# Opening of a token, attention and FFN layer: the first two pairs of sequences in another order, and two vector operations in another form

## The chip, the cores and the metric

One Trainium2 chip, one of its cores. The metric is the device time of one execution in microseconds. The kernel before took 981.53 us as the median of three runs (979.28 to 981.59).

## What is computed

Two layers over 32 sequences of 192 tokens (64 image patches and 128 words), 256 channels, all in float32. The change lies in layer 0 only:

```python
h = concat([patches(x) @ tokW + tokb, table[x_txt]], axis=1)
a = layernorm(h)
q, k, v = a @ wq.T, a @ wk.T, a @ wv.T
h = h + softmax(causal(q @ k.T / 16)) @ v
a = layernorm(h)
h = h + ternary_linear(gelu(ternary_linear(a, w_up)), w_down)
# ternary_linear: x / (rms(x) + eps) times sign(w) * (|w| > 0.5 * mean|w|)
```

Layer 1 (a recurrent mixer and a mixture of experts) follows in the stages B and C of the program and is left alone.

## The kernel before

Stage A (`part_a`) computes layer 0. It takes the sequences two at a time: 16 pairs, numbered 0 to 15 here, each as three tiles of 128 tokens (both sequences' image tokens in one tile, then the words of each). A float32 product is made of products of a high part, rounded to the short format of TensorE, and a low part, the rest: hi times hi, hi times lo, lo times hi (`three`, `product`). So most results leave the accumulator (PSUM) twice: ScalarE (ACT) writes the high part (`hi`), VectorE (DVE) subtracts it for the low part (`lo`). For the patches VectorE makes the high part (`patch_hi`), GpSimd (POOL) the low part (`patch_lo`); for the GELU outputs GpSimd makes the low part (`gelu_lo`, L334).

The steps of a pair are named by kind. In time they come as: `tok` (patch product), `emb` (add the bias, statistics), `root1` (powers on GpSimd), `apply1` (writes x_normed), `xT` (six transposes, "turn"), `x_split`, `t` (times the merged query-key matrix), `t_split`, `score`, `max`, `exp`, `pT`, `v`, `v_split`, `pv`, `h1` (residual and second statistics), `root2`, `scale2` (writes x_normed of the second norm), `x2T`, `x2_split`, `up.0` to `up.7` with `gelu.0` to `gelu.7` and `add.0` to `add.7` (sums of squares), `down.0` to `down.2`, `ss`, `rscale`, `h2`.

One list `order`, written by hand, sets the order on all engines: `run` goes through it once for every step g from -4 to 15, and `offset` says for each kind how many pairs ahead of g it works (tok 2, v and pv 1, up and down 0). Each engine executes its own pieces in that order and waits on semaphores, and never skips a waiting instruction. The steps from -4 to 1 and from 12 to 15 are written out; a loop makes the ones between. The attention of pair 0 falls in step -2, pair 0's probabilities and pair 1's scores in step -1, the FFN of pair 0 in step 0.

The steps before 0 also prepare weights. On VectorE `abs_sum` sums a weight matrix's magnitudes, TensorE adds them over the partitions (`[128 x 1]` product), and `ternary` writes half the mean (`half_alpha`) and then each half of the ternary matrix, in two instructions each (L478, L481), with `gelu_sq` as a scratch tile. `raw_Wl` and `raw_Wv` are the tiles in which the up and down weights lie here. TensorE executes extra transposes of the identity, called fills (L716, table `fill`), ahead of some steps of the opening. ACT_TABLE_LOAD is ScalarE's change between the tables of exp and GELU.

In `patch_load` SyncE (SP) loads the next pair's patches once both halves of the last ones are split. The first down product of pair 0 waits for the whole of the down weights:

```python
if c == 0 and isinstance(n, int) and n == 0:
    pe.wait_ge(s["w_sum"], 4)
```

and pair 1's patches are split on VectorE behind pair 0's statistics and ahead of its `apply1`:

```python
last.then_inc(s["ln_aggr"], 1)
if isinstance(n, int) and n == 0:
    patch_hi(1)
```

## Time and profile before

| | us |
|---|---|
| median of three runs | 981.53 |
| lowest and highest run | 979.28, 981.59 |
| the profiled execution: its own time | 979.7 |
| its span | 977.8 |
| TensorE (PE) busy in the span | 934.9 |
| VectorE (DVE) busy | 791.8 |
| ScalarE (ACT) busy | 594.2 |
| GpSimd (POOL) busy | 545.2 |

The profile covers one execution. A timeline row gives the start and the duration in us, the engine and the line, the tiles written and read, how many equal neighbours it merges (x3), and in brackets how long the engine had stood idle before it and what ended that. Engines followed by q are their queues. Products of TensorE overlap, so that 12 of them can start in 1.5 us though each lasts 0.3.

### The profile page before, as it was taken

The page shows a single profiled execution, that of the slowest core. Times are in us where ns is not written, and L with a number is a line of the kernel's source. Part 1 is how long each engine was busy: PE and PEld are TensorE (multiplying, and loading weights), DVE is VectorE, ACT ScalarE, POOL GpSimd, SP SyncE. Part 2 cuts the span into 40 slices and gives each one's busy share as a digit, 9 for nine tenths or more (in the row PEclk, how much of TensorE's full clock was granted, in tenths as well). Part 3 has the DMA queues.
Part 4 walks back from the last instruction along what each step waited for, and adds up shares of the span by engine and source line. Part 5 has one row for each costly group of instructions (what it writes and reads, how often), then busy time and mean ns, then how long its engine had stood idle before and what let it go on. Part 6 is the DMA issues. An engine that isn't in the chain of part 4 may idle for free. (4 is left out here: it accounts for less than half of the span.)

```text
span 977.8 us, 19833 instructions
## 1 busy us (share of the span) xinstructions
PE 934.9 (96%) x6016; PEld 837.6 (86%) x6016; DVE 791.8 (81%) x2376; ACT 594.2 (61%) x1183; POOL 545.2 (56%) x675
## 2 busy tenths in 40 slices
PE   6889999999999999988899999999999999998998
PEld 6789999999999999875678888888888888877887
DVE  4878877777778777774589999999999989995787
ACT  1366666666666666664666767667767766752442
POOL 4256666666666666444445545455455456552673
PEclk9999999999999999999999999999999999999999
DMA  6001111111111113003799899999999999992310
GB/s 226 17 28 44 45 44 44 43 43 43 43 43 43 43 57 128 17 17 113 94 146 153 151 155 158 153 151 152 167 153 173 180 166 154 153 140 52 121 65 22
DMA packets 63014, 96.35 MB, mean 99 GB/s; under 512 B 12366, under 2 KB 32982, under 8 KB 62294
## 3 DMA queue, kind: packets, MB, share of 16 engines
q1 hardware_dynamic: 61390, 91.19, 50.1%
q0 software_dynamic: 1536, 4.20, 1.5%
q8 instruction: 37, 0.61, 0.3%
q14 instruction: 43, 0.35, 0.2%
q10 hardware_dynamic: 8, 0.00, 0.0%
HBM read 31.91 MB, written 13.11 MB: 46 GB/s over the span
## 5 line engine op out<-in xcount | busy, mean ns | idle before, releaser
L334 POOL TENSOR_TENSOR gelu_lo<-gelu_out,gelu_hi 128x384 fp32r<-128x384 f32 x124 | 146.0, 1205 | 29.2 <-DVE gelu_hi L549 28.7
L1050 POOL TENSOR_TENSOR B_y<-B_scan_in,B_states 128x512 f32<-128x512 f32 x48 | 61.8, 1288 | 84.8 <-ACT B_states L1139 84.8
L752 PE MATMUL psAB<-ternary_down,gelu_hi 128*128 128x256 f32 x384 | 96.9, 291 | 5.3 <-POOL gelu_lo L334 4.5
L688 PE MATMUL psAB<-x2T_hi,ternary_up 128*128 128x384 f32 x256 | 92.7, 362 | 0.8 <-DVE residual L678 0.6
L752 PE MATMUL psAB<-ternary_down,gelu_lo 128*128 128x256 f32 x384 | 93.4, 282 | 0.0
L688 PE MATMUL psAB<-x2T_lo,ternary_up 128*128 128x384 f32 x256 | 86.1, 336 | 0.0
L1317 PE MATMUL psAB<-Win_hi,B_x_hi 128*128 128x512 f32 x192 | 83.5, 435 | 0.0
L752 PEld LDWEIGHTS psAB<-ternary_down,gelu_hi 128*128 128x128 f32 x384 | 72.2, 188 | 9.7 <-POOL gelu_lo L334 8.0
L1062 POOL TENSOR_TENSOR B_decayed_u<-B_scan_in 128x512 f32<-128x512 f32 x48 | 62.1, 1293 | 29.5 <-DMA B_scan_in<-B_stage 28.2
L1235 DVE SCALAR_TENSOR_TENSOR psAB<-B_decayed_u,psAB 128x128 f32<-128x128 f32 x192 | 67.8, 353 | 12.1 <-PE psAB L1329 11.2
L1329 PEld LDWEIGHTS psAB<-B_partial_dots,B_minus_same_batch 128*128 128x128 f32 x384 | 65.3, 191 | 14.3 <-DVE B_partial_dots L1219 4.1
L1317 PE MATMUL psAB<-Win_hi,B_x_lo 128*128 128x512 f32 x192 | 75.5, 393 | 0.0
L1317 PE MATMUL psAB<-Win_lo,B_x_hi 128*128 128x512 f32 x192 | 75.3, 392 | 0.0
L752 PEld LDWEIGHTS psAB<-ternary_down,gelu_lo 128*128 128x128 f32 x384 | 72.5, 189 | 0.0
L1056 POOL TENSOR_TENSOR B_v_scale<-B_half_vv,half_powers 128x1 f32<-128x1 f32 x48 | 26.3, 549 | 78.8 <-ACT B_v_squared L1160 78.8
L403 ACT ACTIVATE gelu_out<-psAB 128x384 f32<-128x384 f32 x128 | 62.7, 490 | 10.2 <-PE psAB L688 9.9
L1219 DVE CUSTOM_DVE_ANT_0 B_products<-B_scan_in,psAB 128x128 f32<-128x128 f32 x192 | 55.2, 287 | 13.4 <-DVE psAB L1235 8.0
L1224 DVE TENSOR_TENSOR psAB<-psAB,B_scan_in 128x128 f32<-128x128 f32 x192 | 57.5, 299 | 6.5
L568 DVE TENSOR_TENSOR gelu_sq_sum<-gelu_sq_sum,gelu_sq 128x384 f32<-128x384 f32 x105 | 61.2, 582 | 1.7
L1329 PE MATMUL psAB<-B_partial_dots,B_minus_same_batch 128*128 128x1 f32 x384 | 54.8, 212 | 3.9 <-DVE B_partial_dots L1219 3.6
L1342 PE MATMUL psAB<-Wout_hi,B_y_hi 128*128 128x256 f32 x192 | 55.6, 290 | 2.7 <-DVE B_y_lo L1279 1.5
L390 ACT ACTIVATE gelu_sq<-gelu_out 128x384 f32<-128x384 f32 x112 | 57.3, 528 | 0.0
(274 smaller groups left out, 3318.2 us busy)
## 6 DMA issues: line engine op xcount, KB each, us to landing
B_scan_in<-B_stage SPq DMA_DIRECT2D x192, 256.0 KB, 6.9
patches<-in_patches SPq DMA_DIRECT2D x16, 384.0 KB, 3.1
B_residual<-layer_out SPq DMA_DIRECT2D x48, 128.0 KB, 4.1
out_dram<-B_residual SPq DMA_DIRECT2D x48, 128.0 KB, 3.7
layer_out<-residual SPq DMA_DIRECT2D x32, 128.0 KB, 1.8
raw_Win<-in_experts SPq DMA_DIRECT2D x3, 768.0 KB, 4.2
raw_Wl<-in_experts SPq DMA_DIRECT2D x3, 768.0 KB, 4.2
layer_out<-residual SPq DMA_DIRECT2D x32, 64.0 KB, 2.0
```

The lines of the kernel that those rows point to most:

```text
L334: nc.gpsimd.tensor_tensor(act_l[:, k, :], act[:, k % DEEP, :], act_h[:, k, :].bitcast(F32), ALU.subtract).then_inc(s["ffn_lo"], 1)
L390: nc.scalar.activation(out, act[:, k % DEEP, :], ACT.Square).then_inc(s["sq_done"], 1)
L403: nc.scalar.activation(act[:, k % DEEP, :], ps[:, 6 + k % 2, 0:GT], ACT.Gelu).then_inc(s["gelu_done"], 1)
L568: nc.vector.tensor_tensor(sqsum[:], sqsum[:], sq[:, k % DEEP, :], ALU.add).then_inc(s["sqsum_done"], 1)
L688: last = nc.tensor.matmul(out, a, b, start=(n == 0), stop=(n == len(terms) - 1))
L752: last = nc.tensor.matmul(ps[:, 6 + k // 2, (k % 2) * D:(k % 2 + 1) * D], x[:, c, k * P:(k + 1) * P], dn_w[:, c, :], start=(c == 0 and x i ...
L1050: nc.gpsimd.tensor_tensor(y[:, j % 2], ring[:, j % R_RING, :, GATE, :], hs[:, j % 2], ALU.mult).then_inc(s["y"], 1)
L1062: nc.gpsimd.tensor_tensor(lu[:, j % 2], ring[:, j % R_RING, :, LAM, :], ring[:, j % R_RING, :, U, :], ALU.mult).then_inc(s["lu"], 1)
L1224: nc.vector.tensor_tensor(state(j, k), state(j, k), ring[:, j % R_RING, k, DRIVE, :], ALU.subtract).then_inc(s["scan"], 1)
L1235: nc.vector.scalar_tensor_tensor(out=state(i, k), in0=lu[:, i % 2, k, :], scalar=dot[:, t % 2:t % 2 + 1], in1=state(i, k), op0=ALU.mult, o ...
L1317: last = nc.tensor.matmul(out, a, b, start=(not biased and ks[0] == 0 and n == 0), stop=(ks[-1] == DC - 1 and n == len(terms) - 1), skip_g ...
L1329: nc.tensor.matmul(dot[:, t % 2:t % 2 + 1], minus[:], part[:, t % 2:t % 2 + 1], start=True, stop=True).then_inc(s["dot"], 1)
```

## The change

- `order_of` gives steps -2, -1 and 0 lists of their own. A third number moves a piece to a later pair. v and v_split of pair 0 now come in step -2 ahead of its scores, those of pair 1 in step -1 ahead of pair 1's scores, and are gone from step 0. The second half of ternary_up and the split of pair 2's patches come later in step -1 than before. x_split of pairs 1 and 2 gets a wait for the scores.
- The sum of the down weights and ternary_down (`abs_down`, `tern_down`) move from step -1 to step 0; the scratch tile of `ternary` is now the weight stage.
- `tok` of pair 0 goes by kind: six hi times hi, six with the patches' low part, six with the weights' low part, each with its own waits. Pair 1's goes to bank 6 and no longer waits for max.
- `emb` of pair 0 takes the statistics of the words ahead of the patches' product.
- The warm-up of the GELU table for pair 0 becomes one of exp.
- x_normed of both norms, in all pairs, and the low parts of the weights (`chunk_lo`) become scalar_tensor_tensor, with the per-token factor as a broadcast second input.
- Other numbers of fills: 46 at the start, then 6, 14, 8, 10, 12 and 6.

```diff
         offset = {...
-                  "abs_down": 1, "tern_down": 1,
+                  "abs_down": 0, "tern_down": 0,
...
+        order_of = {
+            -2: [... """ids_load.0.0 tok.0.0 merge.0.0 patch_load.0.0
...
+            -1: [... """ids_load.0.0 exp.0.0 gelu_table.0.0 pT.0.0
...
+            0: [(w, k, 0) for w, k in order if w not in ("v", "v_split")]}
...
-                for kind, k in order:
-                    off = offset.get(kind, 1)
+                for kind, k, forward in order_of.get(g, ()) if isinstance(g, int) and g in order_of else [
+                        (kind, k, 0) for kind, k in order]:
+                    off = offset.get(kind, 1) + forward
...
-                    nc.scalar.activation(warm_gelu[:], ones[:, 0:1], ACT.Gelu).then_inc(s["gelu_warmed"], 1)
+                    nc.scalar.activation(warm_gelu[:], ones[:, 0:1], ACT.Exp if isinstance(n, int) and n == 0 else ACT.Gelu
+                                         ).then_inc(s["gelu_warmed"], 1)
...
+                    if isinstance(n, int) and n in (1, 2):
+                        sc.wait_ge(s["score_done"], n)
...
+                        v.wait_ge(text_in[sl], 32 * (half + 1))
+                        for i in (1, 2):
+                            nc.vector.bn_stats(stats[:, i, :], emb[:, sl, i, :])
...
-                        last = nc.vector.tensor_scalar(xn[:, i, :], emb[:, sl, i, :], moments[:, i, 0:1],
-                                                       rstd[:, i:i + 1], ALU.subtract, ALU.mult)
+                        last = nc.vector.scalar_tensor_tensor(out=xn[:, i, :], in0=emb[:, sl, i, :],
+                                                              scalar=moments[:, i, 0:1],
+                                                              in1=rstd[:, i:i + 1].to_broadcast([P, D]),
+                                                              op0=ALU.subtract, op1=ALU.mult)
...
-            fill = {("tok", 0): 40, ("xT", 0): 16, ("t", 0): 10, ("score", 0): 10, ("pv", 0): 10, ("xT", 1): 4,
-                    ("t", 1): 10, ("score", 1): 10}
+            fill = {("tok", 0): (46, 6), ("xT", 0): (6, 6), ("t", 0): (14, 6), ("pT", 0): (8, 7), ("pv", 0): (10, 7),
+                    ("t", 1): (12, 7), ("x2T", 0): (6, 7)}
...
+                        pe.wait_ge(s["patch_hi"], 1)
+                        for a, b, ready, parts in ((pat_h, tok_h, s["w_hi"], 2), (pat_l, tok_h, s["patch_lo"], 1),
+                                                   (pat_h, tok_l, s["w_lo"], 2)):
+                            for c in range(KPC):
+                                if c == 0 or (c == 4 and parts == 2):
+                                    pe.wait_ge(ready, 1 + c // 4)
```

VectorE at the end of step -1, before the change: behind the low part of t of pair 1 (ternary_down, then scale2 of pair 0; `ln_roots` are the powers from GpSimd).

```order
L472 TENSOR_SCALAR half_alpha<-psAB 128x1 [waits A_w_alpha_ps]
L478 TENSOR_SCALAR gelu_sq<-raw_Wv,half_alpha 128x1024 [waits A_w_sum,A_w_alpha]
L481 SCALAR_TENSOR_TENSOR ternary_down<-raw_Wv,half_alpha,gelu_sq 128x1024 [waits A_w_sign]
L478 TENSOR_SCALAR gelu_sq<-raw_Wv,half_alpha 128x1024 [waits A_w_sum]
L481 SCALAR_TENSOR_TENSOR ternary_down<-raw_Wv,half_alpha,gelu_sq 128x1024 [waits A_w_sign]
L664 SCALAR_TENSOR_TENSOR ln_den<-ln_roots 128x3 [waits A_ln2_roots]
L667 RECIPROCAL ln_scale<-ln_den 128x3 [waits A_ln2_den]
L671 TENSOR_SCALAR x_normed<-residual,ln_moments,ln_scale 128x256 [waits A_ln2_scale]
```

The same engine in step 0 after the change, from GELU output 0 to the low part of t of pair 2 and on.

```order
L568 CAST gelu_hi<-gelu_out 128x384 [waits A_gelu_done] x2
L655 SCALAR_TENSOR_TENSOR x_normed<-embedded,ln_moments,ln_rstd 128x256 [waits A_xT_done,A_ln_aggr,A_ln_rstd]
...
L484 TENSOR_REDUCE abs_sum_parts<-raw_Wv 128x32 [waits A_tern_in1]
L487 TENSOR_REDUCE abs_sum<-abs_sum_parts 128x1 [waits A_w_abs_parts]
L568 CAST gelu_hi<-gelu_out 128x384 [waits A_gelu_done]
...
L560 TENSOR_TENSOR tT_lo<-psAB,tT_hi 128x768 [waits A_t_hi]
L493 TENSOR_SCALAR half_alpha<-psAB 128x1 [waits A_w_alpha_ps]
L499 TENSOR_SCALAR weight_stage<-raw_Wv,half_alpha 128x1024 [waits A_w_sum,A_w_alpha]
L502 SCALAR_TENSOR_TENSOR ternary_down<-raw_Wv,half_alpha,weight_stage 128x1024 [waits A_w_sign]
L499 TENSOR_SCALAR weight_stage<-raw_Wv,half_alpha 128x1024 [waits A_w_sum]
L502 SCALAR_TENSOR_TENSOR ternary_down<-raw_Wv,half_alpha,weight_stage 128x1024 [waits A_w_sign]
```

The sum of the down weights and ternary_down now stand among the splits of pair 0's GELU outputs and pair 2's attention.

TensorE in step 0 after the change, the waiting products between t of pair 2 and the first down products of pair 0 (psAB is the accumulator).

```order
L719 MATMUL psAB<-xT_hi,qk_hi 128x384 [waits A_emb_img,A_x_lo]
...
L763 MATMUL psAB<-abs_sum,ones 128x1 [waits A_h1_done,A_w_abs]
L789 MATMUL psAB<-ternary_down,gelu_hi 128x256 [waits A_ffn_lo,A_w_sum,A_gelu_done]
L789 MATMUL psAB<-ternary_down,gelu_lo 128x256
L789 MATMUL psAB<-ternary_down,gelu_hi 128x256 [waits A_ffn_lo]
```

The product with abs_sum stood in step -1 before, ahead of pair 1's scores; now it stands directly ahead of the down products.

VectorE in step -2 after the change, from pair 0's patch product to x_normed.

```order
L636 TENSOR_TENSOR embedded<-psAB,patch_bias 128x256 [waits A_tok_done,A_mask_ready,A_const_in]
L641 BN_STATS ln_stats<-embedded 128x6 [waits A_emb_img,A_text_in0]
L646 BN_AGGR ln_moments<-ln_stats 128x2 [waits A_ln_stats]
...
L556 CAST patches_hi<-patches 128x768 [waits A_tok_done,A_patch_in]
L655 SCALAR_TENSOR_TENSOR x_normed<-embedded,ln_moments,ln_rstd 128x256 [waits A_ln_aggr,A_ln_rstd]
```

The cast of pair 1's patches stands where it stood, ahead of x_normed.

## Rows read from the trace of the kernel before

**Rows 1.** A stretch: PE, PEld, DVE, ACT, POOL busy us; granted clock, DMA share, GB/s.
```profile
124.00:408.00 284.00, 280.59 (x2084) 271.79 (x2082) 223.23 (x634) 181.99 (x383) 190.74 (x188) 1.00 0.16 49
```
**Rows 2.** Waits of PE from 80 to 400 us: in total, times, longest.
```profile
PE psAB L752 <- POOL gelu_lo L334: 2.6, 12, 0.3
```
**Rows 3.** Timeline of DVE, around pair 0's first x_normed.
```profile
17.66 0.56 DVE L537 CAST patches_hi<-patches 128x768 fp32r<-128x768 f32 x1 [1.49 <-DMA patches<-in_patches]
18.14 2.56 DVE L628 TENSOR_SCALAR x_normed<-embedded,ln_moments,ln_rstd 128x256 f32<-128x256 f32 x3
```
**Rows 4.** Line L271, the loads of patches, first 60 us.
```profile
DMA to landing us min/median/max: 3.0/3.2/8.5
```
**Rows 5.** Timeline of PE: turns, t, score, down and the turn of pair 1.
```profile
20.75 0.87 PE L699 MATMUL psAB<-ident,x_normed 128*128 128x128 f32 x6 [2.39 <-DVE x_normed L628]
23.52 0.44 PE L688 MATMUL psAB<-xT_hi,qk_hi 128*128 128x384 f32 x1 [0.80 <-DVE xT_lo L541]
27.77 0.39 PE L688 MATMUL psAB<-xT_hi,tT_hi 128*128 128x256 f32 x1 [0.30 <-DVE tT_lo L541]
43.65 0.45 PE L688 MATMUL psAB<-xT_hi,qk_hi 128*128 128x384 f32 x1 [0.80 <-DVE xT_lo L541]
53.57 1.54 PE L699 MATMUL psAB<-ident,x_normed 128*128 128x128 f32 x6 [3.25 <-DVE x_normed L671]
72.75 0.39 PE L752 MATMUL psAB<-ternary_down,gelu_hi 128*128 128x256 f32 x1
77.37 0.87 PE L699 MATMUL psAB<-ident,x_normed 128*128 128x128 f32 x6
```
**Rows 6.** Busy us by engine in one stretch, granted clock behind them.
```profile
53.70:56.50 2.80, 2.80 (x14) 2.80 (x15) 1.52 (x8) 1.35 (x4) 0.00 (x0) 0.50 0.00 0
```
**Rows 7.** The same for the fills (L716) alone: PE, PEld, clock.
```profile
2.00:5.00 3.00, 3.00 (x14) 3.00 (x15) 1.00 0.53 145
6.00:8.00 2.00, 2.00 (x21) 1.98 (x19) 1.00 1.00 313
```
**Rows 8.** Timeline of POOL: patches_lo, the powers of scale2, the first gelu_lo.
```profile
18.30 1.90 POOL L318 TENSOR_TENSOR patches_lo<-patches,patches_hi 128x768 fp32r<-128x768 f32 x1 [0.71 <-DVE patches_hi L537]
46.97 1.78 POOL L359 TENSOR_TENSOR ln_roots<-ln_pair,half_powers 128x6 f32<-128x6 f32 x1
61.95 1.98 POOL L334 TENSOR_TENSOR gelu_lo<-gelu_out,gelu_hi 128x384 fp32r<-128x384 f32 x2
```
**Rows 9.** Line L628, x_normed: duration of one, ns.
```profile
L628 DVE TENSOR_SCALAR x_normed<-embedded,ln_moments,ln_rstd x48: 399/406/1891, 18.1 to 390.7; 128x256 f32<-128x256 f32 x48
```
**Rows 10.** Line L562, scalar_tensor_tensor of the last pair, two inputs in on-chip memory.
```profile
L562 DVE SCALAR_TENSOR_TENSOR gelu_sq_sum<-gelu_sq_sum,gelu_sq x7: 550/558/1371, 437.1 to 445.4; 128x384 f32<-128x384 f32 x7
```
**Rows 11.** Timeline of DVE from 31 to 73 us.
```profile
31.50 0.17 DVE L605 TENSOR_SCALAR neg_max<-row_max 128x3 f32<-128x3 f32 x1
38.41 1.05 DVE L628 TENSOR_SCALAR x_normed<-embedded,ln_moments,ln_rstd 128x256 f32<-128x256 f32 x3
39.38 2.29 DVE L463 TENSOR_REDUCE abs_sum_parts<-raw_Wv 128x32 f32<-128x2048 f32 x1
47.76 0.15 DVE L472 TENSOR_SCALAR half_alpha<-psAB 128x1 f32<-128x1 f32 x1
52.05 0.16 DVE L664 SCALAR_TENSOR_TENSOR ln_den<-ln_roots 128x3 f32<-128x3 f32 x1
58.56 0.42 DVE L610 TENSOR_TENSOR embedded<-psAB,patch_bias 128x256 f32<-128x256 f32 x1
64.76 0.35 DVE L549 CAST gelu_hi<-gelu_out 128x384 fp32r<-128x384 f32 x1
67.60 0.96 DVE L541 TENSOR_TENSOR xT_lo<-psAB,xT_hi 128x768 fp32r<-128x768 f32 x1 [1.01 <-ACT xT_hi L379]
69.77 1.25 DVE L641 SCALAR_TENSOR_TENSOR residual<-psAB,row_inv,embedded 128x256 f32<-128x256 f32 x3
72.24 0.31 DVE L652 BATCH_NORM_AGGREGATE ln_moments<-ln_stats 128x2 f32<-128x6 f32 x3
```

More of the change, by code:

```diff
@@ L145, in flat, with tok_bank @@
             return t[:].rearrange("p a b -> p (a b)")
+        def tok_bank(n):
+            return 6 if isinstance(n, int) and n == 1 else 2
         chunks = []
@@ L606, in piece @@
                 if kind == "emb":
+                    first = isinstance(n, int) and n == 0
+                    if first:
+                        v.wait_ge(text_in[sl], 32 * (half + 1))
+                        for i in (1, 2):
+                            nc.vector.bn_stats(stats[:, i, :], emb[:, sl, i, :])
+                        v.wait_ge(s["const_in"], 16)
+                        v.wait_ge(s["mask_ready"], 1)
                     v.wait_ge(s["tok_done"], n + 1)
                     wait(v, s["h1_done"], n - 1)
-                    nc.vector.tensor_tensor(emb[:, sl, 0, :], ps[:, 2, 0:D], bias_tok[:], ALU.add).then_inc(s["emb_img"], 1)
+                    nc.vector.tensor_tensor(emb[:, sl, 0, :], ps[:, tok_bank(n), 0:D], bias_tok[:],
+                                            ALU.add).then_inc(s["emb_img"], 1)
                     v.wait_ge(text_in[sl], 32 * (half + 1))
                     v.wait_ge(s["emb_img"], n + 1)
-                    for i in range(TILES):
+                    for i in (0,) if first else range(TILES):
                         last = nc.vector.bn_stats(stats[:, i, :], emb[:, sl, i, :])
@@ L670, in piece @@
                     for i in range(TILES):
-                        last = nc.vector.tensor_scalar(xn2[:, i, :], h[:, sl, i, :], moments2[:, i, 0:1],
-                                                       scale2[:, i:i + 1], ALU.subtract, ALU.mult)
+                        last = nc.vector.scalar_tensor_tensor(out=xn2[:, i, :], in0=h[:, sl, i, :],
+                                                              scalar=moments2[:, i, 0:1],
+                                                              in1=scale2[:, i:i + 1].to_broadcast([P, D]),
+                                                              op0=ALU.subtract, op1=ALU.mult)
                     last.then_inc(s["ln2_out"], 1)
@@ L706, in keys @@
                 return x[:, k, :].rearrange("p (t c) -> p t c", t=TILES)[:, 0:3:2, :]
-            fill = {("tok", 0): 40, ("xT", 0): 16, ("t", 0): 10, ("score", 0): 10, ("pv", 0): 10, ("xT", 1): 4,
-                    ("t", 1): 10, ("score", 1): 10}
+            fill = {("tok", 0): (46, 6), ("xT", 0): (6, 6), ("t", 0): (14, 6), ("pT", 0): (8, 7), ("pv", 0): (10, 7),
+                    ("t", 1): (12, 7), ("x2T", 0): (6, 7)}
             def piece(kind, k, n, sl, half):
-                if isinstance(n, int):
-                    for _ in range(fill.get((kind, n), 0)):
-                        nc.tensor.transpose(ps[:, 6, 0:P], ident[:], ident[:])
+                if isinstance(n, int) and (kind, n) in fill:
+                    turns, into = fill[kind, n]
+                    if into == 7:
+                        pe.wait_ge(s["w_alpha"], 1)
+                    for _ in range(turns):
+                        nc.tensor.transpose(ps[:, into, 0:P], ident[:], ident[:])
                 if kind == "merge" and isinstance(n, int) and n == 0:
@@ L734, in piece @@
                             pe.wait_ge(s["w_sum"], 2)
+                            pe.wait_ge(s["emb_img"], 2)
                     else:
```

43 lines of the change are left out of this document (28 added, 15 removed).

## The prediction

> **What bounds the kernel now.** First the busy time by stretches. Between 124 and 408 us TensorE is busy 280.6 of 284 us at the full clock [rows 1], and its only wait there, 2.6 us in 12 pieces, is for the last `gelu_lo` that GpSimd subtracts [rows 2]. So the 14 later pairs stand near TensorE's bound, with 0.2 us a pair set by GpSimd and VectorE. What is left to win lies before 80 us, where a chain runs from engine to engine, so I read the timelines of that stretch next: what each instruction waits for last, and where VectorE stands idle. I number pairs from 0; x_normed(0) is pair 0's. At the end I count along VectorE's queue, since the change fills it.
>
> **Part 1, patch products by kind, bank 6 for pair 1.** The product of pair 0 can begin when its high parts are there and end some 2.5 us earlier. But the next step is not free to follow: VectorE splits pair 1's patches ahead of x_normed(0), and that cast ends an idle wait for a DMA, at 17.66 [rows 3]. The load takes 8.5 us to land, the longest of its four [rows 4], behind the ternary weights on the same engines, and the change moves none of it. So x_normed(0) starts at 18.14 as before: this part is worth 0 while that load holds. Its cost is the idle TensorE behind it. It now has nothing from about 13.6 (46 fills to 8.9, 18 products to 11.1, merge and 6 fills 2.5; an estimate) to 20.8, 7.2 us instead of 2.4 [rows 5]. After the idle 3.3 us ahead of the turn of pair 0's second norm the granted clock was 0.50, the 1.2 GHz level, to 56.6, 3.1 us, and six turns took 1.54 instead of 0.87 us [rows 5, 6]. A turn or fill then takes 0.2 us instead of 0.12. I take the same 3.1 us here: six turns to 22.05, 9.5 of the 14 fills slow, 4.5 fast, so t(0) at 24.5 against 23.52 [rows 5]: **+1.0**. Bounds: 0 if the clock holds, +1.8 if it stays low longer.
>
> Fills are transposes, and 21 ran in the 2 us from 6 us on, 14 in the 3 us from 2 us on, with nothing else on the engine [rows 7]: transposes alone brought the fast rate. The Trainium skill, "TensorE: Matmul & The Clock Gate", Part 4: PE-mode transpose, says that transposes do not count as busy for the clock. By it the low stretch would run on through all of t(0) and the sum would be about 2 us worse; the trace speaks against it, and I go by the row.
>
> **Part 2, tensor_scalar and tensor_tensor become scalar_tensor_tensor.** x_normed(0) takes 2.56 us for three since one sits 1.9 us behind GpSimd's patches_lo [rows 3, 8, 9]. A scalar_tensor_tensor with both inputs in on-chip memory is held in the same way: the seven of the last pair take 0.558 us and one of them 1.371, beside a `gelu_lo` [rows 10]. So I count no relief, and the length only: 0.558 less a third of 384 columns (0.13, from 0.4 for the 384 and 0.155 around them) is 0.425 against 0.406 of now [rows 9, 10], 0.02 each. Bounds: a gain of 1.5 us if GpSimd does not hold it; the same kind takes 1.25 us for three where it reads PSUM (the residual of [rows 11]), against 1.05 for pair 1's x_normed now [rows 11], 0.2 more a step of three. For tokW_lo the answer is the same, and its end is covered by 12 other products.
>
> **Part 3, v(0) ahead of score(0).** From t(0) to score(0) it is 4.25 us now [rows 5]. Then it is t (2.1), the alpha sum (0.3) and 18 value products at 0.12 (2.2), which outlast the split of t: 4.65, so score(0) at 29.15 against 27.77, **+1.4**. In return everything up to t(1) is shorter. neg_max is ready 3.9 us after the score starts (31.67 after 27.77 [rows 5, 11]), 33.05; then v_lo 0.95, and the embedding of pair 1 begins at 34.0; its powers are done 3.4 us on, 37.4 (58.56 to 61.95 [rows 8, 11]); x_normed(1) 1.2, half of ternary_up 2.05, xT_lo 1.0 and t(1) starts at 41.75 against 43.65 [rows 5]: **-1.9**. The two ACT_TABLE_LOADs fall away beside this chain, so they add nothing of their own.
>
> **Part 4, ternary_down and its sum leave the opening.** Now the powers of the second norm end at 48.75, and scale2 starts at 52.05, since 4.3 us of ternary_down stand before it [rows 8, 11]. Without them it starts at 46.9 and x2T(0) at 48.95 behind six fills, against 53.57 [rows 5]: **-4.6**. That is the change's profit, and it is partly kept from pair 2: patches_hi(2) moved behind scale2, so its patches_lo ends at 50.85, the load of the next patches goes out only then, lands 3.2 us later, as the middle ones do [rows 4], and its cast stands ahead of pair 2's embedding on VectorE: 54.6 against 58.56 [rows 11], **-4.0**.
>
> **Part 5, where that work went: VectorE in the first FFN step.** Down(0) on TensorE waits for the last ternary_down. Count VectorE from 54.6. Powers at 58.0. x_normed(2) then waits 1.0 us for the gelu_lo that starts with it (1.98 for two [rows 8]): 60.1. abs_sum of the down weights, 2.29 and 0.2 [rows 11]: 62.6 for gelu_hi 2, now at 64.76. From there to the residual h1(1) it is 5.0 us, 1.5 of them waits that fall away: 66.1 (69.77 now). Its statistics, 2.8 (69.77 to 72.55): 68.9. tT_lo, 0.95: 69.8. ternary_down, 4.3 (47.76 to 52.05): **74.1** [rows 11]. So the lead of 4.0 is spent, since 6.8 us of work joined an engine that is then full. TensorE is done with t(2) at about 67.6 and idle for 6.5 us. It starts down(0) at 74.2. Now it has 36 products left at 72.75 and reaches x2T(1) at 77.37 [rows 5], 0.122 us each with the full clock. Then it has 50: 6.1 us, and 1.25 more for 3.1 us at 0.50 (0.2 us each, 14 in 2.8 us [rows 6]). x2T(1) at 81.5 against 77.37: **+4.2**. Taking v(1) out of this step saves TensorE 2.2 us, all inside that idle time. Nothing later is idle enough to win it back: TensorE waits 0.2 us a pair.
>
> **Part 6, the 14 later pairs.** x_normed of either norm stands in the loop that sets the 0.2 us wait: gelu_hi 2 follows the first, the turn of the second follows the other. At 0.02 each and six a pair that is 0.12; a third of it I take as slack of the turn, so +0.08 a pair, **+1.1** in all. Bounds: -0.3 a pair (TensorE's whole idle share, 3.4 us in 284 [rows 1]) if the hold is gone, +0.38 if each step takes 1.25.
>
> **Sum.** +4.2 +1.1 = +5.3 on the profiled execution: span 977.8 to 983.1, time 979.7 to 985.0. That execution is 1.8 us under the median of the runs, 981.53, so I predict **986.8 us**.
>
> **Rivals.**
> A. *Not slower: the new x_normed runs beside GpSimd unhindered.* Place: the three overlaps (18.3, 58.0, and gelu_lo 1 of each pair). Price: -1.55 at 18.3, -1.0 at 58.0, and TensorE's idle share of 14 pairs, 0.3 each, -4.2, in place of +1.1. 4.2 - 2.55 - 4.2 = -2.55: 979.0. Slower turns into no change once 2.4 us are saved, which the first two places alone would do. For it: the residual of pair 1, of the new kind, took 1.25 us for three [rows 11] while GpSimd was subtracting, but it reads PSUM. Against: the row of 1.371 us. The Trainium skill, "SBUF — State Buffer", Who interferes with whom, says that a VectorE instruction with two SBUF inputs contends with a GpSimd instruction that reads SBUF; by that rule, which that row bears out, A does not come. Chance 0.20.
> B. *The patches of pair 1 land by 14 us.* Then part 1 does bring something: x_normed(0) ends at 16.9, still beside patches_lo(1), everything moves by -3.85, and VectorE's load in the FFN step leaves +0.3 + 1.1: 983.0. Against: issue and bytes are the same. Chance 0.13.
> C. *Each new x_normed is as long as the ones that read PSUM.* 14 x 0.38 = 5.3 instead of 1.1: 991.0. Chance 0.12.
> D. *Low clock through t(0)*, by the rule above: +2.1: 989. Chance 0.05.
> The forecast has 0.50.
>
> **How the numbers follow.** A measurement of this kernel can tell about 0.3%, 2.9 us, from no change: below 978.6 is faster, above 984.4 slower. Of the forecast's 0.50, 0.42 is slower; its 0.08 below the line is the case that the clock holds at 20.8 and 74 (-1.0, -1.25). A: 0.08 faster, 0.12 same. B: 0.03, 0.08, 0.02. C and D: slower. Together faster 0.11, same 0.28, slower 0.61. The range takes in A at its foot, 979.5, and C at its head, 991.5; the forecast alone would be 983.5 to 989.
>
> **What would show it.** patches_hi(1) still at 17.7 behind a DMA, x_normed(0) ending near 20.8; the clock at 0.50 from about 21 to 24; x2T(0) near 49; a VectorE without gaps from 55 to 74; TensorE idle for 6 us ahead of the first down product, with ternary_down as releaser, and the clock low after it; x2T(1) near 81.5; from there on pairs of the present length. I am wrong if down(0) starts before 71, which needs VectorE's embedding of pair 2 before 51.5, or if the later pairs change by more than 0.1 us each.

## The result, and the profile after

The changed kernel takes **992.37 us**, the median of 4 runs (991.01 to 993.97), beside 981.56 us (979.28 to 983.18) of the kernel before on the same chip. The ratio is 1.0108, with a 95% interval of 1.0083 to 1.0133: slower by 10.6 us, and slower than the range of the prediction reached. One run of e15 below, 1131 us long at a granted clock of 0.75, was in a slower state and is left out of all medians and ratios. The profiled execution took 991.01 us, its span is 988.9 against 977.8 us. The lines of the code have moved: x_normed of the first norm is L655, of the second L700, the split into low parts L560, the casts of the GELU L568, ternary L499 and L502, the turns L730, the products L719 and the down products L789.

The timeline of PE after: the turns of the first two pairs, the first product of t(1), of t(2) and of down(0). Columns: start us, duration us, engine, line, operation, tiles, shape, count, and in brackets the idle time before with what ended it.

```profile
21.14 1.54 PE L730 MATMUL psAB<-ident,x_normed 128*128 128x128 f32 x6 [7.13 <-DVE x_normed L655]
...
40.44 0.82 PE L730 MATMUL psAB<-ident,x_normed 128*128 128x128 f32 x6
...
43.21 0.44 PE L719 MATMUL psAB<-xT_hi,qk_hi 128*128 128x384 f32 x1 [0.64 <-DVE xT_lo L560]
...
50.36 0.82 PE L730 MATMUL psAB<-ident,x_normed 128*128 128x128 f32 x6
...
62.07 0.87 PE L730 MATMUL psAB<-ident,x_normed 128*128 128x128 f32 x6 [1.04 <-DVE x_normed L655]
68.70 0.69 PE L719 MATMUL psAB<-xT_hi,qk_hi 128*128 128x384 f32 x1 [3.46 <-DVE xT_lo L560]
78.57 0.55 PE L789 MATMUL psAB<-ternary_down,gelu_hi 128*128 128x256 f32 x1 [6.11 <-issue]
...
86.04 0.82 PE L730 MATMUL psAB<-ident,x_normed 128*128 128x128 f32 x6
```

Against [rows 5] it reads: xT(0) 0.4 us later, t(1) 0.4 us earlier, x2T(0) 3.2 us earlier, and x2T(1), the last row, 8.7 us later. All of that 8.7, and the 3.2 besides, goes between 50 and 86 us: 3.5 us of idle TensorE ahead of t(2), and 6.1 ahead of the first down product, which the profile puts down to no engine ("issue").

The timeline of DVE after tells what it was:

```profile
17.79 0.56 DVE L556 CAST patches_hi<-patches 128x768 fp32r<-128x768 f32 x1 [2.46 <-DMA patches<-in_patches]
18.27 2.82 DVE L655 SCALAR_TENSOR_TENSOR x_normed<-embedded,ln_moments,ln_rstd 128x256 f32<-128x256 f32 x3
...
48.31 1.27 DVE L700 SCALAR_TENSOR_TENSOR x_normed<-residual,ln_moments,ln_scale 128x256 f32<-128x256 f32 x3
...
55.63 0.42 DVE L636 TENSOR_TENSOR embedded<-psAB,patch_bias 128x256 f32<-128x256 f32 x1
...
59.23 2.79 DVE L655 SCALAR_TENSOR_TENSOR x_normed<-embedded,ln_moments,ln_rstd 128x256 f32<-128x256 f32 x3
61.94 2.27 DVE L484 TENSOR_REDUCE abs_sum_parts<-raw_Wv 128x32 f32<-128x2048 f32 x1
...
65.09 1.15 DVE L568 CAST gelu_hi<-gelu_out 128x384 fp32r<-128x384 f32 x1
...
66.63 1.15 DVE L568 CAST gelu_hi<-gelu_out 128x384 fp32r<-128x384 f32 x1
67.70 0.94 DVE L560 TENSOR_TENSOR xT_lo<-psAB,xT_hi 128x768 fp32r<-128x768 f32 x1
...
69.20 1.26 DVE L670 SCALAR_TENSOR_TENSOR residual<-psAB,row_inv,embedded 128x256 f32<-128x256 f32 x3
...
73.23 0.96 DVE L560 TENSOR_TENSOR tT_lo<-psAB,tT_hi 128x768 fp32r<-128x768 f32 x1 [1.24 <-ACT tT_hi L396]
...
77.19 1.29 DVE L502 SCALAR_TENSOR_TENSOR ternary_down<-raw_Wv,half_alpha,weight_stage 128x1024 fp32r<-128x1024 f32 x1
```

The last half of ternary_down ends at 78.48 and down(0) starts at 78.57. The busy time and the clock by stretches, TensorE alone (stretch, its length, busy us and instructions, granted clock, DMA share, GB/s):

```profile
14.00:17.00 3.00, 0.01 (x1) 0.98 0.85 339
17.00:21.00 4.00, 0.00 (x0) 0.50 0.01 2
21.00:24.00 3.00, 2.86 (x14) 0.50 0.66 194
24.00:27.00 3.00, 3.00 (x13) 0.50 0.09 30
27.00:28.00 1.00, 1.00 (x7) 0.93 0.00 0
...
68.00:71.00 3.00, 2.30 (x7) 0.52 0.01 3
71.00:74.00 3.00, 1.46 (x8) 0.91 0.01 3
74.00:78.00 4.00, 0.00 (x0) 0.62 0.13 36
78.00:81.00 3.00, 2.43 (x11) 0.50 0.13 40
```

The clock falls while TensorE is idle at 17 us, and TensorE then works at the 1.2 GHz level for 6 us from 21 on, and for some 3 us each behind the wait that begins at 65 us and the one that ends at 78.6.

The rest of the loss is in the later pairs. Of x_normed there, first after, then before: the groups of VectorE between 130 and 400 us (count, then busy us, mean ns, idle before).

```profile
L655 DVE SCALAR_TENSOR_TENSOR x_normed<-embedded,ln_moments,ln_rstd 128x256 f32<-128x256 f32 x30 | 16.5, 602 | 0.0
L700 DVE SCALAR_TENSOR_TENSOR x_normed<-residual,ln_moments,ln_scale 128x256 f32<-128x256 f32 x33 | 14.1, 481 | 0.4
```

```profile
L628 DVE TENSOR_SCALAR x_normed<-embedded,ln_moments,ln_rstd 128x256 f32<-128x256 f32 x33 | 14.8, 501 | 0.0
L671 DVE TENSOR_SCALAR x_normed<-residual,ln_moments,ln_scale 128x256 f32<-128x256 f32 x30 | 10.6, 410 | 0.4
```

And the waits of PE from 80 to 410 us, where [rows 2] has 2.6 us in 12:

```profile
PE psAB L789 <- POOL gelu_lo L351: 4.6, 10, 0.5
PE psAB L719 <- DVE xT_lo L560: 1.4, 2, 0.7
```

Measured from turn to turn of the second norm, pairs 1 to 14 (13 steps), a pair takes 25.36 us against 25.10. I use these two numbers for every run below: x2T(1), the start of the turn of pair 1's second norm, which takes in the whole opening, and the length of a later pair.

### The profile page after: what moved, and what is told of

It is laid out like the page before. It is cut to its first block and busy times, and to the rows that moved or that the text cites. A ratio compares the mean times of both kernels' runs of the same rounds, so it can differ in the third digit from the quotient of the medians.

```text
span 988.9 us, 19815 instructions
## 1 busy us (share of the span) xinstructions
PE 934.7 (95%) x6008; PEld 838.1 (85%) x6008; DVE 808.2 (82%) x2376; ACT 593.3 (60%) x1181; POOL 540.9 (55%) x675
## 5 line engine op out<-in xcount | busy, mean ns | idle before, releaser
L351 POOL TENSOR_TENSOR gelu_lo<-gelu_out,gelu_hi 128x384 fp32r<-128x384 f32 x124 | 144.0, 1187 | 36.6 <-DVE gelu_hi L568 36.1
L789 PE MATMUL psAB<-ternary_down,gelu_hi 128*128 128x256 f32 x384 | 98.2, 293 | 13.5 <-POOL gelu_lo L351 6.6
L789 PE MATMUL psAB<-ternary_down,gelu_lo 128*128 128x256 f32 x384 | 94.7, 284 | 0.0
L719 PE MATMUL psAB<-x2T_hi,ternary_up 128*128 128x384 f32 x256 | 92.8, 363 | 1.2 <-DVE residual L709 0.6
L789 PEld LDWEIGHTS psAB<-ternary_down,gelu_hi 128*128 128x128 f32 x384 | 73.3, 191 | 17.3 <-POOL gelu_lo L351 9.5
L719 PE MATMUL psAB<-x2T_lo,ternary_up 128*128 128x384 f32 x256 | 86.2, 337 | 0.0
L1366 PE MATMUL psAB<-Win_hi,B_x_lo 128*128 128x512 f32 x192 | 75.5, 393 | 0.0
L1111 POOL TENSOR_TENSOR B_decayed_u<-B_scan_in 128x512 f32<-128x512 f32 x48 | 62.2, 1295 | 22.3 <-DMA B_scan_in<-B_stage 12.4
L789 PEld LDWEIGHTS psAB<-ternary_down,gelu_lo 128*128 128x128 f32 x384 | 73.5, 191 | 0.0
L420 ACT ACTIVATE gelu_out<-psAB 128x384 f32<-128x384 f32 x128 | 62.6, 490 | 12.5 <-PE psAB L719 10.6
L475 ACT ACTIVATE x2T_hi<-psAB 128x768 fp32r<-128x768 f32 x16 | 13.0, 813 | 81.6 <-PE psAB L730 81.6
L1378 PE MATMUL psAB<-B_partial_dots,B_minus_same_batch 128*128 128x1 f32 x384 | 54.6, 211 | 3.8 <-DVE B_partial_dots L1268 3.5
```

Of the source, the lines that this page charges most:

```text
L351: nc.gpsimd.tensor_tensor(act_l[:, k, :], act[:, k % DEEP, :], act_h[:, k, :].bitcast(F32), ALU.subtract).then_inc(s["ffn_lo"], 1)
L420: nc.scalar.activation(act[:, k % DEEP, :], ps[:, 6 + k % 2, 0:GT], ACT.Gelu).then_inc(s["gelu_done"], 1)
L719: last = nc.tensor.matmul(out, a, b, start=(n == 0), stop=(n == len(terms) - 1))
L789: last = nc.tensor.matmul(ps[:, 6 + k // 2, (k % 2) * D:(k % 2 + 1) * D], x[:, c, k * P:(k + 1) * P], dn_w[:, c, :], start=(c == 0 and x i ...
L1111: nc.gpsimd.tensor_tensor(lu[:, j % 2], ring[:, j % R_RING, :, LAM, :], ring[:, j % R_RING, :, U, :], ALU.mult).then_inc(s["lu"], 1)
L1366: last = nc.tensor.matmul(out, a, b, start=(not biased and ks[0] == 0 and n == 0), stop=(ks[-1] == DC - 1 and n == len(terms) - 1), skip_g ...
```

## The experiments

I held three theories. **T1:** ternary_down and its sum in the first FFN step hold down(0) back. **T2:** the new form of x_normed costs the later pairs. **T3:** x_normed(0) behind the cast of patches(1) leaves TensorE idle, and the low clock after it makes t(0) late. Each ratio is against the kernel before, timed beside it; the median of before was 979.8 to 982.0 us in these groups of runs, so the ratios compare and the medians of different rows only roughly. x2T(1) and the pair are read from one execution each. The same kernel gave x2T(1) at 73.51 and 74.18 (e8, e15) and at 74.52 and 73.56 (e12, e16), so a difference of less than 1 us in that column says little.

| run | x2T(1), us | a later pair, us | median, us | ratio and interval |
|---|---|---|---|---|
| before | 77.37 | 25.10 | 981.6 | 1 |
| changed | 86.04 | 25.36 | 992.4 | 1.0108 (1.0083 to 1.0133) |
| e1, ternary_down back | 81.48 | 25.37 | 987.7 | 1.0075 (1.0049 to 1.0100) |
| e2, tensor_scalar back | 85.53 | 25.10 | 988.5 | 1.0077 (1.0052 to 1.0102) |
| e3, long fill | 86.77 | 25.38 | 991.4 | 1.0116 (1.0089 to 1.0143) |
| e4, cast behind | 83.99 | 25.38 | 989.4 | 1.0088 (1.0062 to 1.0113) |
| e5, before, new form | 78.98 | 25.33 | 986.0 | 1.0061 (1.0042 to 1.0081) |
| e6, e1 + e2 + e4 | 78.15 | 25.09 | 979.9 | 0.9994 (0.9977 to 1.0010) |
| e7, before, cast behind | 78.50 | 25.10 | 979.7 | 0.9992 (0.9975 to 1.0009) |
| e8, before, late half, fill | 73.51 | 25.10 | 976.8 | 0.9967 (0.9953 to 0.9982) |
| e9, e6 laid apart | 76.03 | 25.11 | 977.5 | 0.9956 (0.9938 to 0.9973) |
| e10, e9 with the short fill | 76.94 | 25.10 | 977.2 | 0.9959 (0.9941 to 0.9976) |
| e11, sum of down back | 86.16 | 25.33 | 992.3 | 1.0104 (1.0078 to 1.0131) |
| e12, e8 without the fill | 74.52 | 25.10 | 975.5 | 0.9931 (0.9904 to 0.9958) |
| e13, whole tile as input | 79.38 | 25.35 | 986.3 | one run |
| e14, one pointer scalar | 76.98 | 24.99 | 977.0 | one run |
| e15, e8 again | 74.18 | 25.10 | 976.0 | 0.9946 (0.9928 to 0.9964) |
| e16, e12 again | 73.56 | 25.11 | 976.3 | 0.9952 (0.9939 to 0.9966) |

### The three causes, one at a time (e1 to e4)

e1 puts ternary_down back into step -1, as before; its `[128 x 1]` product goes with it and no longer waits for the residual:

```diff
-    t_split.0.0 v.0.1 score.0.0 scale2.0.0      (step -1)
+    t_split.0.0 tern_down.0.1 tern_down.1.1 v.0.1 score.0.0 scale2.0.0
-    tern_up.1.-1 pv.0.0
+    tern_up.1.-1 abs_down.0.1 pv.0.0
```

> The changed kernel with ternary_down and its sum of magnitudes put back into step -1, everything else as changed. T1 (these five VectorE instructions in step 0 hold the first down product back): x2T(0) starts at about 57 us instead of 50.4, but down(0) no longer waits at 72 to 78.5, and x2T(1) comes at about 79 us instead of 86.0; the time falls by 6 to 8 us, to about 985. T2 (the new form of x_normed alone costs the time, 3.5 us over the steady pairs) and T3 (the long low clock behind x_normed(0)) leave x2T(1) at 85 us or later and the time within 1.5 us of 992.4.

x2T(1) came at 81.48: 4.6 of the 8.7 us, not 7, and the time fell by 0.33 points, 3.2 us. x2T(0) was at 55.61, 5.2 later than in the changed kernel, and down(0) at 75.5. T1 holds, for a little over half of the loss at x2T(1) and a third of the lost time; the 6 to 8 us that I expected were too much. e2 undoes the form in both norms (`tensor_scalar(xn, emb, moments, rstd, subtract, mult)` again):

> The changed kernel with tensor_scalar and its two pointer scalars back in both x_normed, everything else as changed. T2 (the form is slower by itself): the three instructions take 1.28 us again instead of 1.5 or more in the steady pairs, the pair from x2T to x2T goes from 25.36 to 25.10 us, and the time falls by 3.3 to 3.9 us, to about 988.8. Rival (the steady pair is longer for another reason, such as the phase in which the first pairs leave the queues): the pair stays at 25.3 or more and the time within 1 us of 992.4. What my prediction said of this, 0.08 us a pair, would give a fall of 1.1 us.

The pair is at 25.10 again, x2T(1) 0.5 us earlier, the time 0.31 points lower, 3 us. The first down product came 1.6 us earlier (77.00), but the granted clock behind it was at 0.50 until 82.6 us, 5.6 us on, where in the changed kernel it was so for 3.2 us (78.6 to 81.8), and TensorE took 8.5 us from there to x2T(1) instead of 7.5. T2 holds, and the length of the steady pair has no other cause. e4 moves one call:

```diff
                 last.then_inc(s["ln_aggr"], 1)
-                if n == 0: patch_hi(1)
...
             (apply1) last.then_inc(s["ln_out"], 1)
+                if n == 0: patch_hi(1)
```

> The changed kernel with the cast of patches(1) behind x_normed(0) on VectorE instead of ahead of it, everything else as changed. T3 (x_normed(0) waits behind a cast that waits for a transfer): x_normed(0) starts at about 15.3 us instead of 18.3 and takes 1.3 to 1.5 us instead of 2.8, as GpSimd is not yet on patches_lo(1); TensorE is idle for 2.5 us instead of 7, t(0) starts about 4 us earlier and the time falls by 3 to 4 us, to about 989. Rival (patches(1) is then what is late: its products end later and emb(1) takes the gain back): x_normed(1) at 38.7 us as now, and the time within 1 us of 992.4.

xT(0) came 3.1 us earlier, at 18.03, and x2T(1) 2.05 earlier; the time fell by 0.2 points, 2 us. Here too the first down product gained more, 3.0 us (75.52), but the clock was at 0.50 until 81.0 us and 8.5 us lay behind it instead of 7.5. In the timeline of DVE of e4 the wait for GpSimd has moved with the order, to wv_lo, 0.68 us long in the changed kernel:

```profile
16.70 1.28 DVE L653 SCALAR_TENSOR_TENSOR x_normed<-embedded,ln_moments,ln_rstd 128x256 f32<-128x256 f32 x3 [1.45 <-POOL ln_rstd L361]
17.89 0.55 DVE L556 CAST patches_hi<-patches 128x768 fp32r<-128x768 f32 x1
18.36 0.68 DVE L605 SCALAR_TENSOR_TENSOR qk_lo<-psAB,qk_hi 128x512 fp32r<-128x512 f32 x1
18.96 1.94 DVE L549 SCALAR_TENSOR_TENSOR wv_lo<-weight_stage,wv_hi 128x512 fp32r<-128x512 f32 x1
```

So the order takes x_normed off the load and off GpSimd, but VectorE has as much to do. e3 tests the other half of T3, `("xT", 0): (58, 6)` in place of `(6, 6)`:

> The changed kernel with 58 instead of 6 transposes of the fill ahead of xT(0), so that TensorE stays busy from 14.0 to about 21 us, while VectorE casts patches(1) and writes x_normed(0). T3 (the idle stretch brings the low clock, and transposes count as activity): the granted clock stays at the high level through t(0), t(0) starts 2 to 2.5 us earlier, and as the attention of step -2 is a chain, x2T(0) comes 1.5 to 2.5 us earlier; the time falls by 1 to 2.5 us. Rival (transposes don't hold the clock, as the Trainium skill says in "TensorE: Matmul & The Clock Gate", Part 4): the clock is at the low level from 17 to 27 us as now, and the time within 0.5 us of 992.4.

The stretches of PE of e3:

```profile
14.00:18.00 4.00, 4.00 (x39) 1.00 0.63 243
18.00:20.00 2.00, 2.00 (x20) 1.00 0.01 2
20.00:22.00 2.00, 0.09 (x1) 1.00 0.00 0
22.00:24.00 2.00, 1.83 (x17) 1.00 0.69 206
24.00:26.00 2.00, 1.64 (x12) 1.00 0.40 123
```

The clock stays at the full level over the whole of t(0), behind 58 transposes and nothing else from 13.6 to 20.1 us and 2.1 us of idle time. That is one execution, and no sure hold: in e9 below, 28 transposes to 16.1 us and 2.0 us of idle time ahead of xT(0) were followed by a stretch at 0.50, while the turns and the 14 fills behind them ran.

```profile
18.00:22.00 4.00, 3.81 (x20) 0.62 0.01 3
```

But there, as in e6 and e11, the clock came back to 1.00 (at 22.3, 21.8 and 25.2 us) before the first product of t(0) (22.97, 22.44, 25.74), when TensorE had executed only transposes since its wait. The hold in e3 and these returns go against the rule of the Trainium skill that I had weighed ("TensorE: Matmul & The Clock Gate", Part 4), though in the changed kernel the clock came back only 1.8 us into the products of t(0). And the time of e3 did not move. x2T(0) gained 0.9 us, and then the statistics of embedded(2) waited 2.0 us for the rows of its text (0.3 in the changed kernel), so that x2T(1) was at 86.77. The clock of the opening, which my Part 1 priced at 1 us, could be bought back and was worth nothing while that transfer and VectorE's queue stood behind it.

### The form alone, and all three together (e5, e6)

> The kernel before with nothing changed but the form: scalar_tensor_tensor with the broadcast input in both x_normed, in all 16 pairs. T2 (the form costs the steady pairs, and about the same in the opening): x2T(1) at 77.4 to 78.2 us, the pair at 25.36 instead of 25.10 us, and the time 3.3 to 4.5 us over that of before. Rival (the form costs only where the new order of the opening has put it beside GpSimd's work): under 1 us over that of before.

The kernel before with the new form alone is 0.61% slower, 6.0 us. In its profiled execution I find 1.6 by x2T(1), 13 x 0.23 = 3.0 in the steady pairs, and 1.5 in the last pair, of which more at the end. That is more than the 3 us that e2 gave back in the new opening, but the first is good to some 2 us and the second to 3.5, so the difference isn't shown.

> The changed kernel with three things put back or out of the way at once: both x_normed on tensor_scalar, the cast of patches(1) behind x_normed(0), ternary_down and its sum in step -1. If the causes are apart (T1, T2 and T3 hold side by side) their gains at x2T(1) add, 4.6 and 2.1 us and some 0.5 us of the form from 86.0 us, to 78.9 us, the pair is 25.10 us, and the time 10 to 11 us under that of the changed kernel, 0 to 1.5 us over that of before. Rival (they share one wait, so that the second removal finds little left): x2T(1) at 80.5 us or later, the time 3 us or more over that of before.

With all three in, the kernel is at the time of before (0.9994), x2T(1) 7.9 us earlier than in the changed kernel and 0.8 later than before. The single gains at x2T(1) were 4.6, 0.5 and 2.05, 7.1 us. Within the 1 us of that column they add, so they are three causes and not one wait seen three times. Two of them take a part of the change back. The third doesn't: the cast stands ahead of x_normed(0) in the kernel before as well, where moving it gains nothing (e7). The changed kernel with e1 and e2 alone wasn't run, so it isn't shown that those two parts of the change make up its whole loss. What is left of the change in e6 (products by kind, bank 6, values ahead of scores, no change of tables) brings no gain: xT(1) is at 37.09 instead of 40.94, and the waits of PE between 30 and 60 us say where that lead ends:

```profile
PE psAB L715 <- DVE xT_lo L560: 2.5, 1, 2.5
PE psAB L726 <- DVE x_normed L698: 2.3, 1, 2.3
PE psAB L715 <- POOL patches_lo L335: 1.5, 1, 1.5
```

### Where VectorE's work can stand (e7 to e12, e15, e16)

> The kernel before with the cast of patches(1) behind x_normed(0), nothing else. T3's wait is in this kernel too (the cast waits for its transfer at 17.66 us and stands ahead of x_normed(0)): x_normed(0) at about 17 us and 1.05 us long, its turns at about 18 instead of 20.75, and the time 2 to 3 us under that of before. Rival (the opening has other chains of the same length behind it, such as the raw weights' transfers and the products of pair 1, so that the attention of pair 0 gains nothing further on): x2T(1) within 0.7 us of 77.4 and the time within 1 us of before.

No gain. The profile is that of the slowest of its twelve runs (983.63 us). In it the products of pair 0 ended 0.75 us later than before, since the granted clock was at 0.50 from 11.6 us on (from 12.3 in before), and wv_lo took the hold as in e4. xT(0) was at 19.49; e12 and e16, with the same instructions up to there, had it at 18.03 and 18.07, without a low clock in those products. At x2T(0) 0.2 us were left, and the low clock there lasted to 59.3 us instead of 56.6. By the medians of 12 and 29 runs the cast alone is worth nothing here.

e8 adds two things: the second half of ternary_down behind the row maxima of pair 1, and 14 transposes ahead of x2T(0). The scratch tile of ternary moves to the weight stage with it. e12 is e8 without the transposes.

```diff
-    tern_up.0 tern_down.0 tern_down.1 add.4
+    tern_up.0 tern_down.0 add.4
-    x2T down.2 max tern_up.1
+    x2T down.2 max tern_down.1 tern_up.1
-    tern_tmp = sq[...]
+    tern_tmp = stage[:, 0:1024]
```

> The kernel before with the cast behind x_normed(0), the second half of ternary_down behind the row maxima of pair 1 instead of ahead of x_normed2(0) (its scratch in the weight stage), and 14 transposes ahead of x2T(0), so that TensorE doesn't stand idle there. If VectorE's chain to x_normed2(0) and the low clock behind its wait set the opening: x2T(0) 2 us earlier than in the run with the cast alone, no 0.50 clock at its turns (1.5 us in before), x2T(1) 2 to 3 us earlier, and the time 4 to 6 us under that of before. Rival (what comes behind, VectorE's queue of step -1 and 0, is as full as before, so the half is only moved): as the run with the cast alone, within 1 us.

> The kernel before with the cast behind x_normed(0) and the second half of ternary_down behind the row maxima of pair 1, but without the 14 transposes ahead of x2T(0). If the gain of the run with both is from the half (VectorE's order), x2T(1) is within 1 us of its 73.5 us and the time 2 to 3 us under that of before; if it is from the clock that the transposes hold, the clock is 0.50 for 3 us from about 50 us on, x2T(1) at 75 us or later and the time within 1.5 us of before.

Both are faster than before, 0.33% and 0.69%: 3.1 us where I had said 4 to 6 for e8, 6.1 where I had said 2 to 3 for e12. As e7 is no faster than before, the gain comes with the late half; the half without the cast wasn't run. The DVE timeline of e12 shows what it does: the second norm stands between the halves, and starts 2.8 us earlier than before. First e12, then the kernel before:

```profile
48.06 1.28 DVE L481 SCALAR_TENSOR_TENSOR ternary_down<-raw_Wv,half_alpha,weight_stage 128x1024 fp32r<-128x1024 f32 x1
...
49.67 1.06 DVE L671 TENSOR_SCALAR x_normed<-residual,ln_moments,ln_scale 128x256 f32<-128x256 f32 x3
...
52.65 1.28 DVE L481 SCALAR_TENSOR_TENSOR ternary_down<-raw_Wv,half_alpha,weight_stage 128x1024 fp32r<-128x1024 f32 x1
```

```profile
52.46 1.06 DVE L671 TENSOR_SCALAR x_normed<-residual,ln_moments,ln_scale 128x256 f32<-128x256 f32 x3
```

The turn at 50.78 has an idle time of 1.14 us before it instead of 3.25, and the clock there is at its full level without any transposes. To learn whether the transposes add something, both were timed again side by side:

> The kernel of e8 once more, beside that of e12: before, with the cast behind, the late half and 14 transposes ahead of x2T(0). If the clock at x2T(0) is worth what it showed in the profiles (x2T(1) 73.51 against 74.52 us): 1 us under e16. Otherwise within 0.5 us of e16.

> The kernel of e12 once more: before, with the cast behind and the late half, no transposes ahead of x2T(0). The time 3 to 6 us under that of before, as in e12 (6.1) and e8 (3.1 with the transposes).

976.0 and 976.3 us, 0.9946 and 0.9952: they add nothing that can be seen. This version, e16, beats both kernels: 5.6 us under before (0.48%, interval 0.34 to 0.61).

e9 lays the changed kernel's work out in the same way: e6, with the sum behind xT_lo(1), the first half behind the row maxima, the second behind v_lo(1), and longer fills, 28 ahead of xT(0) and 14 ahead of x2T(0). e10 has the six of the changed kernel ahead of xT(0) again, which its expectation calls none.

> The run with all three put back, with VectorE's work for ternary_down laid into its idle stretches instead of ahead of what TensorE waits for: the sum of magnitudes behind xT_lo(1), the first half behind the row maxima of pair 1, the second behind v_lo(1); besides 28 transposes (6 before) ahead of xT(0) and 14 (6) ahead of x2T(0). T1 in its strict form (what counts is not that VectorE does this work but which operand stands behind it): TensorE's 2.5 us ahead of t(1) and 2.3 us ahead of x2T(0) go, and with them the low clock at 42 to 46 us and 55 to 59 us; x2T(1) at 73 to 75 us instead of 78.15, the time 3 to 5 us under that of before. Rival (VectorE is full from 15 to 78 us, so what is moved is only paid elsewhere): x2T(1) at 77 us or later and the time within 1 us of before.

> The same kernel as e9 without any transposes ahead of xT(0). If transposes hold TensorE's clock over VectorE's wait (as the granted clock of 1.00 from 14 to 30 us in the run with 58 of them shows), the clock here is 0.50 for some 4 us from 17 us on, and x2T(1) and the time are 1 to 2 us later than in e9. Rival (VectorE's chain sets the start of t(0) and what follows at either clock): within 0.5 us of e9.

x2T(1) fell by 2.1 us against e6, to 76.03, and the time is 0.44% under before: the forecast of 3 to 5 us held, though x2T(1) is 1 us later than I said. TensorE's waits ahead of t(1) and x2T(0) went from 2.5 and 2.3 us to 0.6 and none. The time of e10 is the same within 0.3 us, so the rival holds for the fills once more. Its clock was not low from 17 us on as forecast, but from 23.4 to 26.8, under the products of t(0). The new order, at its best here, is no faster than the old order at its best (977.5 to 976.3): I find nothing that the change's reordering itself brings.

> The changed kernel with only the sum of magnitudes for ternary_down (2.46 us of VectorE) moved from step 0 to step -1, behind xT_lo(1); ternary_down itself stays in step 0. T1: VectorE has no idle time between x_normed(2) and h1(1) in step 0, so ternary_down ends about 2.4 us earlier than 78.5, less what x2T(0) is later; x2T(1) at 84 to 84.5 us instead of 86.0, the time 1.5 to 2 us under that of the changed kernel. Rival (down(0) waits for ternary_down's place behind tT_lo(1), whose chain through ScalarE sets it, not for VectorE's time): x2T(1) within 0.5 us of 86.0.

A miss. With only the 2.46 us of the sum taken out of step 0, x2T(1) was at 86.16 and the time as before that edit. xT(1) stood 0.3 us earlier than in the changed kernel, but x2T(0) 1.5 later, since the sum now stood ahead of the residual of pair 0. So ternary_down ended at 77.5, only 1 us earlier, and the low clock behind the wait for it, to 83.2 us, took that. Moving a part of the work ahead of the chain pays in one step what it saves in the other. T1 in its plain form, that the sum counts by its length wherever it stands, is wrong; what counts is the operand that stands behind it.

### What the form costs (e13, e14)

> The kernel before with scalar_tensor_tensor in both x_normed as in e5, but with the whole tile of the patch bias (128x256) as its second tensor in place of the broadcast column. It leaves out the division by the root of the variance in both norms. If a second tensor read costs (whatever its stride): 481 ns mean for x_normed2 in the steady pairs as in e5, the pair at 25.33 us. If it is the broadcast of one column that is slow: about 410 ns and 25.10 us.

> The kernel before with the constant 1.0 in place of the second pointer scalar of tensor_scalar in both x_normed. It leaves out the division by the root of the variance in both norms. If tensor_scalar takes the same whatever its scalars are: 410 ns mean for x_normed2 in the steady pairs and 2.56 us for the three of pair 0 beside GpSimd's patches_lo, the pair at 25.10 us. If the second pointer is what makes it wait beside GpSimd: the three of pair 0 in 1.05 to 1.3 us.

The group of the second norm in e13, and in e14:

```profile
L673 DVE SCALAR_TENSOR_TENSOR x_normed<-residual,ln_moments,patch_bias 128x256 f32<-128x256 f32 x31 | 13.3, 482 | 0.4
```

```profile
L671 DVE TENSOR_SCALAR x_normed<-residual,ln_moments 128x256 f32<-128x256 f32 x30 | 8.8, 349 | 0.4
```

So in the steady pairs 128x256 fp32 in on-chip memory takes 349 ns with one pointer scalar, 410 with two, 481 with a second tensor, be it a broadcast column or a whole tile. The pair follows: 24.99, 25.10 and 25.33 to 25.36 us. The Trainium skill, "VectorE: DVE Perf Modes", Mode 2×_2P, says that an instruction with one tensor input can read it through both ports and one with two cannot; that the kind of second tensor makes no difference agrees with it. Beside GpSimd the shorter form is held all the same: the three of pair 0 took 2.42 us in e14, 2.56 before, 2.82 after.

## Why the prediction failed, point by point

The sign and the places were right: slower, by a VectorE without gaps in step 0, an idle TensorE ahead of down(0), and a small loss in each later pair. Both terms of the sum were too small: +4.2 at x2T(1) against +8.7 measured, and +1.1 against +3.4 over 13 pairs. The last pair added 0.2. The span grew by 11.1 us, so the later layers gave 1.1 back. Of the 5.8 us that the forecast of the span fell short, the larger part, 4.5, is the term of Part 5, VectorE's queue up to the first down product; 2.3 is the term of Part 6, which rests on the length that Part 2 put on the new form.

- **Part 1** was right that the product by kind is worth nothing while the cast waits for its load (17.79, 18.27), and mis-sized the clock. I let it be low for 3.1 us from the turn on, as behind the 3.3 us wait [rows 6]. It fell at 17 us, in the idle time, and stayed low for 6 us of work: t(0) at 25.3, +1.8 and my upper bound, where I took +1.0. That size differs between profiles with the same work on TensorE there, from the turn at which it starts: 6.0 us here, 5.0 in e4, 4.6 in e1, 4.2 in e2 and 3.1 in e11. So my 3.1 was the least of them. e3 shows that this term is worth nothing in the time. Of the rivals, B fell with the load, for which the cast waited to 17.8 us, and D came in part: the clock was low into the first products of t(0).
- **Part 2** is the step that was furthest off for its size. I took the length of a scalar_tensor_tensor from seven of 384 columns [rows 10], less a share for the columns, 0.425 us. It is 0.481, 71 ns over tensor_scalar, not 20. I had the 1.25 us for three of [rows 11] as the bound and it was the value: 1.27, the condition of rival C. That no relief comes from GpSimd was right (2.82 us at 18.27), and rival A falls.
- **Part 3** held in its steps: from t(0) to score(0) 5.4 us where I had 4.65, as the first products of t(0) still ran at the low clock, and the rest nearly as written (its terms add up to 41.65, not 41.75); t(1) at 43.21, a gain of 0.4 us where I had 1.9.
- **Part 4** held in size: x2T(0) at 50.36, 3.2 us earlier than before where I had 4.6, the difference being that of t(1).
- **Part 5** had the mechanism, and its length of VectorE's queue is the term that was mis-sized most: 4.4 us lost on the way. My times against the measured ones: embedded(2) 54.6 and 55.6, x_normed(2) ended 60.1 and 61.9, h1(1) 66.1 and 69.2, tT_lo 68.9 and 73.2, ternary_down ended 74.1 and 78.5. x_normed(2) began 1.2 us late, behind an embedded(2) that was 1.0 late, and took 2.79 us beside gelu_lo where I had 2.1. Between x_normed(2) and h1(1) I let 1.5 us of waits fall away from the old queue. But two casts of the GELU, 0.35 us each before, took 1.15 each beside gelu_lo (65.09, 66.63), which takes that 1.5 back. And behind the statistics tT_lo waited 1.24 us for ScalarE, a wait that I put at nothing and that the kernel before has at the same place:

```profile
73.85 0.96 DVE L541 TENSOR_TENSOR tT_lo<-psAB,tT_hi 128x768 fp32r<-128x768 f32 x1 [1.29 <-ACT tT_hi L379]
```

  It did not fall away because t(2) itself was late: TensorE stood 3.5 us ahead of it, for xT_lo behind the sum and the casts, and ran it at the low clock. I had counted VectorE alone and taken TensorE's product of that step as covered. From down(0) to x2T(1) it is 7.5 us as measured, 7.35 as predicted.
- **Part 6** had the loop right: gelu_hi later, the wait for gelu_lo 4.6 us instead of 2.6 [rows 2]. With 71 to 101 ns on each of six instructions, 0.5 us of VectorE a pair, the pair grew by 0.26, three times my 0.08. Rival C (0.38) was the nearest of the cases, and its total of 991.0 us is 1.4 under the measured time; I gave it 0.12. That its total came so near is luck in part: it had the opening too short, at +4.2, and the pair too long.

The 0.3% of a measurement plays no part: the loss is three times that. e6 shows that the three causes together give the whole of it back, and e1, e2 and e4 their shares alone: 3.2, 3 and 2 us by the ratios, each good to some 3.5. No single one is clear of that, though every run of e1 and e2 and all but one of e4 lie under the lowest run of the changed kernel (991.01). So that they give more together than apart (11 us against 8 by the ratios, 7.9 against 7.1 at x2T(1)) may be noise. What stays open is why e7 gained nothing where e4 gained 2 us, and how much of T3 belongs to the change.

## What to carry over

Work taken out of one engine's chain must be followed to the queue it joins: ask what operand stands behind it there, and whether the engine that waits is then another one. Splitting such work around the one short instruction that TensorE waits for (e12, e16, with the cast behind as well) gave what moving it all could not. And a form of instruction inside the steady loop is priced by the nearest row of the same shape; its cost is paid 16 times, while an opening is paid once.
